# Moving the turning of the feed-forward weights and the second biases into the first layer's last group of heads

## What is computed

```
def _dequant(w_int, dtype):
    return w_int.astype(dtype) * jnp.asarray(SCALE, dtype)
...
x = x + _L0_attn_a_ref(_layernorm(x, axis=-1), L0_attn_a_Wqkv, L0_attn_a_bqkv, L0_attn_a_Wout, L0_attn_a_bout)
x = x + _L0_ffn_ref(_layernorm(x, axis=-1), L0_ffn_w_gate, L0_ffn_w_up, L0_ffn_w_down)
x = x + _L0_attn_b_ref(_layernorm(x, axis=-1), L0_attn_b_W_qkv, L0_attn_b_b_qkv, L0_attn_b_W_out, L0_attn_b_b_out)
x = x + _L0_ffn_ref(_layernorm(x, axis=-1), L0_ffn_w_gate, L0_ffn_w_up, L0_ffn_w_down)
```

## Time and profile before

| | us |
|---|---|
| three runs, median (lowest to highest) | 1374.61 (1371.66 to 1381.24) |
| the profiled execution, whole | 1372.5 |
| its span in the profile | 1370.7 |

### The profile page before, as it was taken

How to read it: one execution, slowest core, us unless ns; L and a number is a source line. 1 busy time by engine, 2 the same in 40 slices (tenths; PEclk the granted TensorE clock), 3 DMA queues, 4 the chain that set the end, 5 groups by cost and what they waited for, 6 DMA issues and landing times.

```text
span 1370.7 us, 26878 instructions
## 1 busy us (share of the span) xinstructions
PE 1322.5 (96%) x9681; PEld 678.7 (50%) x9681; DVE 1180.1 (86%) x2979; ACT 1010.7 (74%) x1813; POOL 141.6 (10%) x309
## 2 busy tenths in 40 slices
PE   9899999999999999999997988999999999999898
PEld 6544444444444444444435764555555555555477
DVE  8799999999999999999935987788888888888376
ACT  8688888888888888888885542677677767777643
POOL 5620000000000000000001211100000000000011
PEclk9699999999999999999999996899999999999999
DMA  7611101111101111101000433121112211220001
GB/s 215 187 33 32 28 6 32 33 32 33 27 8 32 33 33 33 29 6 33 2 1 1 117 99 93 40 57 33 34 33 55 43 34 34 46 51 2 3 24 39
DMA packets 40060, 58.44 MB, mean 43 GB/s; under 512 B 7796, under 2 KB 19448, under 8 KB 39928
## 3 DMA queue, kind: packets, MB, share of 16 engines
q1 hardware_dynamic: 39928, 56.72, 17.2%
HBM read 36.77 MB, written 18.87 MB: 41 GB/s over the span
## 4 chain that ended last, share of the span: by engine, by line
PE 83%; DVE 7%; ACT 5%; issue 3%; SPq 1%; DMA 1%; POOL 0%; DVEq 0%; ACTq 0%; POOLq 0%
PE psum L1141 28%; PE psum L1077 24%; PE psum L1107 16%; ACT probs L630 4%; PE psum L1005 3%; PE psum L1228 3%; DVE maxima L859 3%; PE psum L1212 2%; PE psum L1115 2%; PE psum L1016 1%; DVE hid L935 1%; PE psum L1157 1%; PE psum L1054 1%; DVE junk L856 1%; PE psum L990 1%
## 5 line engine op out<-in xcount | busy, mean ns | idle before, releaser
L630 ACT ACTIVATE probs<-psum 128x512 f32<-128x512 f32 (+3 forms) x1408 | 833.8, 659 | 213.3 <-PE psum L1107 110.0
L859 DVE TENSOR_REDUCE maxima<-psum 128x1 f32<-128x512 f32 x1232 | 773.6, 682 | 31.5 <-PE psum L1077 25.8
L1077 PE MATMUL psum<-kop,qop 62*128 62x512 f32 (+3 forms) x1744 | 561.6, 437 | 7.0 <-DVE maxima L856 1.5
L1107 PE MATMUL psum<-qop,kop 64*128 64x512 f32 (+3 forms) x1792 | 525.1, 422 | 9.1 <-ACT probs L630 3.3
L1077 PEld LDWEIGHTS psum<-kop,qop 62*128 62x128 f32 x1744 | 267.0, 188 | 376.9 <-DVE maxima L859 285.2
L1141 PE MATMUL psum<-probs,v 128*32 128x512 f32 (+3 forms) x3584 | 440.4, 563 | 0.7 <-ACT probs L630 0.7
L1107 PEld LDWEIGHTS psum<-qop,kop 64*128 64x128 f32 x1792 | 268.3, 188 | 79.3 <-ACT probs L630 46.6
L856 DVE CUSTOM_DVE_ANT_0 junk<-psum,mask 128x384 bf16<-128x384 f32 (+3 forms) x512 | 232.1, 485 | 52.0 <-PE psum L1077 50.0
L1141 PEld LDWEIGHTS psum<-probs,v 128*32 128x32 f32 x3584 | 71.0, 109 | 100.9 <-issue 69.9
L1115 PE MATMUL psum<-half_ident,key_mask 64*128 64x64 bf16 x1024 | 89.0, 197 | 0.0
L523 POOL TENSOR_TENSOR att<-att_raw,rden 128x128 f32<-128x128 f32 x64 | 26.1, 407 | 511.2 <-DVE rden L888 511.2
(11 more groups left out here) (102 smaller groups left out, 749.0 us busy)
## 6 DMA issues: line engine op xcount, KB each, us to landing
qop<-q_parts SPq DMA_DIRECT2D x256, 64.0 KB
kop<-k_parts SPq DMA_DIRECT2D x64, 128.0 KB
kop<-k_parts SPq DMA_DIRECT2D x128, 64.0 KB
q_parts<-parts SPq DMA_DIRECT2D x24, 256.0 KB, 2.9
k_parts<-parts SPq DMA_DIRECT2D x24, 256.0 KB, 3.1
x<-in_L_attn_a_x SPq DMA_DIRECT2D x8, 256.0 KB, 4.5
q_parts<-att SPq DMA_DIRECT2D x8, 256.0 KB, 3.6
k_parts<-att SPq DMA_DIRECT2D x8, 256.0 KB, 3.7
```

The source lines that it names most:

```text
L630: nc.scalar.activation(probs[:, slot, heads[0] % 2:heads[-1] % 2 + 1, c0:], psum[:, bank:bank + len(heads), c0:], ACT.Exp, scale=SCORE_SCA ...
L859: nc.vector.tensor_reduce(dst, src, AX_X, ALU.max).then_inc(ring_free, 1)
L1077: mm(psum[:, bank, 0:width], qop[rows, buf, f, r, qb * P:(qb + 1) * P].bitcast(F32R), kop[rows, buf, r, kh * CHUNK:kh * CHUNK + width].bit ...
L1107: ins = mm(psum[:, bank + k, c0:], kop[rows, buf, c // 2, j * P:(j + 1) * P].bitcast(F32R), qop[rows, buf, f, c // 2, c0:].bitcast(F32R), ...
```

## The change

`wflt` moves from `probs` into `hid`. TensorE turns the three matrices after the last score of steps 5, 6 and 7 of the first layer's last group and spreads the second biases after that of step 8. ScalarE copies the matrices after the last exponential of steps 6, 7 and 8 and the biases after that of step 8. In the diff the first `early_chunk` is ScalarE's, the second TensorE's. Bank 4 replaces banks 2 and 7. The wait for all five copies moves from the walk's first unit to `transpose_ot` at step 9.

```
-        wflt = early[:, wsize:2 * wsize].rearrange("p (k c d) -> p k c d", k=3, c=FB)
+        wflt = hid[:].rearrange("p c q -> p (c q)")[:, 0:wsize].rearrange("p (k c d) -> p k c d", k=3, c=FB)
...
+WEIGHTS_AT, BIASES_AT = (5, 6, 7), 8
...
                 def early_chunk(i):
+                    if layer == 0 and i - 1 in WEIGHTS_AT:
+                        take_weights(WEIGHTS_AT.index(i - 1))
+                    if layer == 0 and i == BIASES_AT:
+                        take_biases(1)
...
                     if kind == "job" and number in plan.paired and number % 2 == 0:
                         clip(number // 2)
-                        if number // 2 in (9, 13, 17):
-                            take_weights(number // 8 - 2)
-                        if number // 2 == 18:
-                            take_biases(1)
...
                 def early_chunk(i):
+                    if layer == 0 and i in WEIGHTS_AT:
+                        pe.wait_ge(ring_free, job_base + plan.jobs_all)
+                        pe.wait_ge(wflt_ready, 2)
+                        transpose_weights(WEIGHTS_AT.index(i))
+                    if layer == 0 and i == BIASES_AT:
+                        pe.wait_ge(setup_ready, 4)
+                        spread_biases(1)
                     if i == plan.project_at[0]:
                         pe.wait_ge(ring_free, job_base + plan.jobs_all)
+                        if layer == 0:
+                            pe.wait_ge(setup_ready, 5)
                         transpose_ot(0, 4)
...
                     if kind == "job":
                         run_job(layer, w, what, number)
-                        if layer == 0 and number in (12, 20, 28):
-                            pe.wait_ge(wflt_ready, 2)
-                            transpose_weights(number // 8 - 1)
-                        if layer == 0 and number == 32:
-                            spread_biases(1)
...
                         if layer == 0 and number == 0:
-                            pe.wait_ge(setup_ready, 5)
                             pe.wait_ge(masks_ready, 1)
```

More of the change, by code:

```diff
@@ L569, in take_biases @@
                 act.wait_ge(setup_psum, (1, 5)[l])
-                nc.scalar.copy(bqk[:, l], psum[:, 7, 2 * E:2 * E + 2])
-                nc.scalar.copy(bvo[:, l].rearrange("p t e -> p (t e)"), psum[:, 7, 0:2 * E]).then_inc(setup_ready, 1)
+                bank = (7, 4)[l]
+                nc.scalar.copy(bqk[:, l], psum[:, bank, 2 * E:2 * E + 2])
+                nc.scalar.copy(bvo[:, l].rearrange("p t e -> p (t e)"), psum[:, bank, 0:2 * E]).then_inc(setup_ready, 1)
             def normalise_first(n):
@@ L674, in copy_ffn_xt, with take_weights @@
                     nc.scalar.copy(ffn_xt[:, 0].bitcast(F32R), psum[:, bank, :]).then_inc(xt_ready[1], 1)
+                def take_weights(k):
+                    act.wait_ge(setup_psum, 2 + k)
+                    dst = gate_up_w[:, k].bitcast(F32R) if k < 2 else down_w[:]
+                    nc.scalar.copy(dst.rearrange("p c d -> p (c d)"), psum[:, 4, 0:HIDDEN]).then_inc(setup_ready, 1)
                 def early_chunk(i):
+                    if layer == 0 and i - 1 in WEIGHTS_AT:
+                        take_weights(WEIGHTS_AT.index(i - 1))
+                    if layer == 0 and i == BIASES_AT:
+                        take_biases(1)
                     if i == plan.project_at[0] - 1:
@@ L686, in early_chunk @@
                         copy_ot(1, 5)
[L688 to L691, removed]
                 def clip(pair):
@@ L994, in spread_biases @@
             def spread_biases(l):
+                bank = (7, 4)[l]
                 pe.wait_ge(wqkv_ready[l], 1)
                 for t in range(2):
-                    mm(psum[:, 7, 2 * E + t:2 * E + t + 1], bias_row[0:1, l, t, :], ones[0:1, 0:1], start=True, stop=True)
-                mm(psum[:, 7, 0:E], ones[0:1, :], bias_row[0:1, l, 2, :], start=True, stop=True)
-                mm(psum[:, 7, E:2 * E], ones[0:1, :], bias_row[0:1, l, 3, :], start=True, stop=True).then_inc(setup_psum, 1)
+                    mm(psum[:, bank, 2 * E + t:2 * E + t + 1], bias_row[0:1, l, t, :], ones[0:1, 0:1], start=True, stop=True)
+                mm(psum[:, bank, 0:E], ones[0:1, :], bias_row[0:1, l, 2, :], start=True, stop=True)
+                mm(psum[:, bank, E:2 * E], ones[0:1, :], bias_row[0:1, l, 3, :], start=True, stop=True).then_inc(setup_psum, 1)
             spread_biases(0)
@@ L1041, in transpose_weights @@
                 for c in range(FB):
-                    ins = nc.tensor.transpose(psum[:, 2, c * P:(c + 1) * P], wflt[:, k, c, :], ident[:])
+                    ins = nc.tensor.transpose(psum[:, 4, c * P:(c + 1) * P], wflt[:, k, c, :], ident[:])
                 ins.then_inc(setup_psum, 1)
```

## The result

| | us |
|---|---|
| before, 20 runs, median | 1373.99 |
| changed, 20 runs, median (lowest to highest) | 1380.49 (1376.59 to 1385.04) |
| ratio changed to before | 1.0042, 95% interval 1.0029 to 1.0054 |
| changed, profiled execution and its span | 1382.95, 1381.1 |

The ratio is +5.8 us (4.0 to 7.4) on the median of before: slower, and clear of the noise, though within the 1% that the prediction called no change. +4.0 was forecast. One of the 20 runs before took 2691.9 us; it is left out of the ratio.

What follows compares the result with a forecast made beforehand. Engine busy shares (TensorE 96%) were held to say little; two short stretches, before the first score and the last group, have their own limits. -1.0 + 5.0 = +4.0 us gives 1376.5 profiled, 1378.6 for the median; predicted 1378, range 1371 to 1385.

Steps and rivals of the forecast that it cites:

- Part one, removed work: Paired stretch before the first score: turning removed, pairs end 5.0 us earlier, first score gains 1.0 us.
- SyncE is late next: Before the first score: SyncE's issues of the maxima stay near 60 us behind fourteen load issues, though maxima are ready sooner.
- The term of -1.0: First score: 0.8 us from maxima landing at 63.0 plus 0.2 for one job finished earlier; ends 0 and -1.8.
- the two landings worked out from the page: Maxima DMAs before the first score: landing at 62.7 or 63.4, counted from the second issue's start or end.
- Part two, the hand-overs: First layer's last group: turning added there, TensorE and ScalarE waiting on each other, +5.0 us; ends 0 and 6.0.
- the three marks: Last group: next score after the first hand-over 1.85 us late, sum from 703.70 2.98 late, gathering of heads 5.0 late.
- the walk: Last group from step 6's last score at 699.93, followed through three hand-overs to the gathering's end at about 711.2.
- The rival: Last group: granted clock falls to 1.2 GHz, about 9.6 us more over seven steps, giving 1388; chance 0.12.
- the argument against: Last group: some 4.4 us of TensorE work in 7.5 us from 700.15, far more than where the clock fell.
- the prediction's own signs of being wrong: SyncE's maxima issues near 55, last group as long as before, or granted clock under 1.00 between 700 and 730.
- costless hand-overs: Last group: turning and copies fall into existing waits, -1.0 + 0.2 = -0.8 us, giving 1373.8; chance 0.12.
- the whole gain of 5.0 us: Paired stretch: maxima sent as soon as turned, -5.0 + 5.0 = 0, giving 1374.6; chance 0.10.

Runs made afterwards that it cites:

- the kernel with the maxima first: Changed kernel with SyncE sending the first half's turned maxima ahead of the second group's fourteen loads; ratio to before 1.0012.
- part one alone: Against the kernel before, turning left out of both the paired stretch and the last group, GpSimd copying matrices and biases unturned; ratio 0.9987.
- bare stops: Changed kernel (1.0042 to before), one turning everything at both places (1.0043), and changed with SyncE sending the maxima ahead of the fourteen loads (1.0012).
- the one with VectorE's copies: Changed kernel with SyncE sending the maxima ahead of the fourteen loads and the last group's four copies on VectorE; ratio to before 0.9966.

## Why the prediction was right, and by how much its terms were off

*Part one, removed work.* The pairs end 4.7 us earlier; 5.0 was worked out. That SyncE is late next and eats it is shown by the 4.76 us wait, and by the kernel with the maxima first, which gets it back. The term of -1.0 came out at -0.6 on average, within its ends of 0 and -1.8, and at +0.3 in the changed kernel's own trace, just outside them; no run shows it clear of the noise. Its weak step was to take the end of the microsecond with traffic, 63.0, for the landing, 3.0 us after the first issue. The waiting scores start 3.5 to 4.6 us after it; in the changed kernel it starts at 65.35, which less 0.92 is 64.4. The 2 us of the Trainium skill (DMA: Bandwidth & Descriptors, anatomy of one DMA) are a figure for DMAs that GpSimd issues, and these are SyncE's. Counted from the end of the second issue, the trace of part one alone comes near it: 60.83 + 1.42 + 2.0 = 64.25, and the score started at 64.55. Over the five waiting traces the score starts 2.1 to 3.2 us after that end, 3.2 in the changed kernel, so the two landings worked out from the page (62.7 and 63.4) were too early as well.

*Part two, the hand-overs.* Forecast 1.85, 2.98 and 5.0 us late at the three marks; measured 1.85, 2.97 and 5.01. Every duration in the walk had been read from the same stretch, and its steps hold one by one: the third copy ends at 709.61 + 0.47 - 0.92 = 709.16, for which the walk had 709.23. So this agreement is not luck. That nothing behind gives it back held as well.

*The clock.* The rival gave it 9.6 us for seven steps if it fell; the argument against was the 4.4 us of work in 7.5. It fell, which was one of the prediction's own signs of being wrong (a granted clock under 1.00 between 700 and 730), in all three traces with bare stops, but for under 4 us instead of seven steps, with TensorE busy throughout (712 to 716), and cost 0.7. The argument that failed is that the clock holds because the stretch in which it had been seen to fall was far emptier: here it fell behind 8.16 us of work in 12. The term that this mis-sized is part two: +5.75 instead of +5.0, the fallen clock put at nothing.

*The sum.* -0.6 + 5.75 = +5.1 by the traces, 0.3 + 5.7 = 6.0 with the changed kernel's own start, +5.8 (4.0 to 7.4) by the runs, +4.0 forecast. Both terms were off the same way, the gain too large and the price too small, so the forecast lies at the edge of the interval. Of the rivals, costless hand-overs are refuted by B; the whole gain of 5.0 us needs another order on SyncE.

## What to carry to other kernels

Work that two engines pass to and fro costs what stands in the queue in front of each hand-over, not only its own duration: here 1.9 us of copies and 2.4 us of products cost 5.0 us with the waits and 1.6 without them, and an idle engine for the copies, or a bank for each, took most of it away. Before work is taken out of a stretch, look up the queue that its result goes through; if what is issued there is ordered behind something else, the order has to change in the same step or nothing is gained. Two changes that each look worthless alone (the removal at the start, the order on SyncE) were worth 4 to 5 us together in the changed kernel, and 2.4 by the trace in the one with VectorE's copies.

## What was not expected of the hardware

The granted clock fell after a stretch in which TensorE was busy for 8.16 of 12 us with stops of 1.06 to 1.63 us, in three traces of three; with the stops filled by products of a unit matrix it stayed at 1.00. The same two small DMAs took between 3.5 and 4.6 us from their first issue to the first score that waits for them (60.85 to 64.39 with the stops filled, 60.71 to 65.35 in the changed kernel), with the same fourteen loads ahead of them. That moves the first score by a microsecond from trace to trace.
